# Expert results added into the residual in memory by indirect transfers, instead of stored, gathered back and combined

## The reference, cut to what matters

```
x = x + gnn(layernorm(x)) + attention(layernorm(x))
h = layernorm(x)                                 # 1250 x 1024
w, e = top2(router(h))                           # two experts of 8 for every token, with weights
x = x + sum over k of w[:, k] * expert[e[:, k]](h)
```

## Time and profile before

| | us |
|---|---|
| runs shown | 3441.88, 3448.74, 3455.16 (median 3448.74) |
| the profiled execution, its own time | 3453.75 |
| its span, first to last instruction | 3452.0 |
| PE busy, PE weight loads | 3101.3 (90%), 2834.2 (82%) |
| DVE, ACT, POOL busy | 2116.8, 1290.2, 401.6 |
| mean granted TensorE clock | 0.941 of full speed |

### The profile page before, as it was taken

The page is one execution under the profiler, slowest core; times in us unless marked ns, Lnnn a source line. Parts: engine busy times, 40 slices in busy tenths (PEclk is TensorE's granted clock), DMA queues, the critical chain, the costliest instruction groups (busy, mean ns, idle before and its releaser), DMA issues.

```text
span 3452.0 us, 52667 instructions
## 1 busy us (share of the span) xinstructions
PE 3101.3 (90%) x21876; PEld 2834.2 (82%) x21876; DVE 2116.8 (61%) x3710; ACT 1290.2 (37%) x2211; POOL 401.6 (12%) x302
## 2 busy tenths in 40 slices
PE   6999999989998799999489999989998999969992
PEld 6897797479987398888389997989998999968882
DVE  6985377977875744434556555776264734646664
ACT  4462055544421034333244334444044413325551
POOL 1044443442000100000300000000000000010002
PEclk9999999999998899999699999999999999969996
DMA  7322123122032156534641000452321432248777
GB/s 248 106 54 40 1 62 92 1 48 68 13 88 88 46 158 190 173 128 152 187 142 38 26 27 30 122 146 76 81 88 48 115 72 81 63 133 267 258 257 228
DMA packets 284267, 366.09 MB, mean 106 GB/s; under 512 B 52472, under 2 KB 234782, under 8 KB 282224
## 3 DMA queue, kind: packets, MB, share of 16 engines
q1 hardware_dynamic: 165035, 203.54, 20.0%
q0 software_dynamic: 51248, 68.03, 8.5%
q10 hardware_dynamic: 67717, 90.69, 8.1%
HBM read 285.75 MB, written 83.74 MB: 107 GB/s over the span
## 4 chain that ended last, share of the span: by engine, by line
PE 55%; DVE 4%; DMA 2%; ACT 2%; issue 1%; ACTq 1%; POOL 1%; POOLq 0%; DVEq 0%; SPq 0%
PE PV L459 12%; PE PV L460 12%; PE PV L461 12%; PE PV L563 6%; PE PS L459 3%; PE PS L461 3%; PE PS L460 3%; DMA b<-y_d,gidx 1%; PE PA L594 1%; PE PA L487 1%; DVE b L1848 1%; DVE b_split L1634 1%; ACTq L121 1%; ACT b L1248 1%; PE PA L878 1%
## 5 line engine op out<-in xcount | busy, mean ns | idle before, releaser
L459 PE MATMUL PV<-WH,b_split 128*125 128x256 f32 (+2 forms) x3708 | 1091.1, 294 | 124.6 <-DVE b_split L1634 107.7
L460 PE MATMUL PV<-WH,b_split 128*125 128x256 f32 (+2 forms) x3708 | 1077.4, 291 | 0.0
L461 PE MATMUL PV<-WH,b_split 128*125 128x256 f32 (+2 forms) x3708 | 1076.4, 290 | 0.0
L1634 DVE TENSOR_TENSOR b_split<-b,b_split 128x500 fp32r<-128x500 f32 x1040 | 687.4, 676 | 435.5 <-ACT b_split L1237 422.4
L1237 ACT CAST b_split<-b 128x500 fp32r<-128x500 f32 x1040 | 626.0, 612 | 808.8 <-PE PV L461 733.4
L459 PEld LDWEIGHTS PV<-WH,b_split 128*125 128x125 f32 (+2 forms) x3708 | 703.6, 190 | 149.7 <-issue 105.8
L460 PEld LDWEIGHTS PV<-WH,b_split 128*125 128x125 f32 (+2 forms) x3708 | 706.5, 191 | 9.9
L461 PEld LDWEIGHTS PV<-WH,b_split 128*125 128x125 f32 (+2 forms) x3708 | 703.0, 190 | 11.3
L1617 DVE TENSOR_TENSOR WH<-WS,WH 128x1024 fp32r<-128x1024 f32 x292 | 344.3, 1221 | 145.7 <-ACT WH L1222 144.4
L1222 ACT CAST WH<-WS 128x1024 fp32r<-128x1024 f32 x292 | 292.1, 1051 | 180.4 <-PE PV L563 143.4
L459 PE MATMUL PV<-b_split,WH 128*128 128x250 f32 (+3 forms) x1136 | 336.9, 297 | 9.2 <-DVE b_split L1634 6.4
(11 more groups left out here) (271 smaller groups left out, 3775.4 us busy)
## 6 DMA issues: line engine op xcount, KB each, us to landing
WS<-in_L_ffn_w SPq DMA_DIRECT2D x46, 1024.0 KB, 6.8
WH<-at_d SPq DMA_DIRECT2D x15, 1093.8 KB
WS<-in_L_ffn_gate_w SPq DMA_DIRECT2D x16, 1024.0 KB, 5.4
WS<-in_L_ffn_up_w SPq DMA_DIRECT2D x16, 1024.0 KB, 6.1
WS<-in_L_ffn_down_w SPq DMA_DIRECT2D x16, 1024.0 KB, 5.1
y_d<-b ACTq DMA_DIRECT2D x60, 256.0 KB
y_d<-b ACTq DMA_DIRECT2D x64, 196.0 KB
b<-key_d POOLq DMA_DIRECT2D x4, 2560.0 KB, 9.4
```

The source lines that it names most:

```text
L459: pe.matmul(o, a[0], b[0], start=start, stop=False, **kw)
L460: pe.matmul(o, a[0], b[1], start=False, stop=False, **kw)
L461: return pe.matmul(o, a[1], b[0], start=False, stop=stop, **kw)
L1634: ve.tensor_tensor(lo, src, hi.bitcast(F32), ALU.subtract).then_inc(xl_done, 1)
```

## The change

It does these things:

- `y_d`, the gathers L1202, `combine` and the result stores L1393 go. So do the four result buffers, the fill of `y_d` on SP's queue (L1020 to L1022), `store_x2` and the output stores at the end.
- The residual is first stored to memory: `store_normed` also stores each residual tile to `acc[layer]`, which is `x2_d` in layer 0 and the output itself in layer 1 (20 more issues on ACT's queue per layer).
- Results are weighted as they leave PSUM: DVE (`tensor_scalar`) and ACT (`activation` with a scale) multiply by `wslot`, the weight of each slot, into a ring of eight tiles of 4 KB a row, which takes the residual's place in SBUF.
- POOL adds each whole tile into `acc[layer]` by an indirect transfer with an add. It waits for both halves of the tile and for the landing of the previous transfer, since two slots may hold the same token. Empty slots go to 128 spare rows behind the tokens.
- The gather for block b + 2 now stands on POOL ahead of the adds of block b and behind those of block b - 1. In layer 1's conditional blocks POOL also waits for each block's last add and gather to land.
- `row_tokens` gets 20 more matmuls (plain float32) for `wslot`, and six more DVE instructions around them for that and for `sidx`, the target rows.
- In layer 0 ACT waits for all adds and loads the residual back into SBUF in ten transfers, and `ln_x2` waits for its group's load instead of combining.

The diff, cut to its core:

```diff
@@ -342,18 +344,14 @@
-        def y_slot(layer, n):
-            s = n % YRING[layer]
-            if layer == 1:
-                at = B3 + s * D
-            elif s >= 4:
-                return rbf[0:R, (s - 4) * D:(s - 3) * D]
-            elif n < 12:
-                at = B1 + (6 + s) * D
-            else:
-                at = (PTO, PTO + D, B1 + 8 * D, B1 + 9 * D)[s]
-            return F[0:R, at:at + D]
+        def y_number(layer, b, t):
+            return b * 4 + t if layer == 0 else E * 4 + b * 2 + t
+        def y_tile(layer, n):
+            at = (B3, B1)[layer] + n % YRING * D
+            return F[:, at:at + D]
@@ -576,7 +574,13 @@
                 mm.then_inc(v_full, 1)
-                mark["rows", layer] = v.n
+                bank = v.take(pe)
+                pe.wait_ge(weight_hot_ready, layer + 1)
+                for n in range(2 * NT):
+                    mm = pe.matmul(bank[0:r, 0:blocks * tiles], at_row[:, n, :].bitcast(F32),
+                                   at_weight[:, n, :], start=(n == 0), stop=(n == 2 * NT - 1))
+                mm.then_inc(v_full, 1)
+                mark["weights", layer] = v.n
@@ -1017,9 +1021,6 @@
-            for r0 in range(FIXED[1] * 256, BLK * 256, 1024):
-                r1 = min(r0 + 1024, BLK * 256)
-                sp.dma_start(y_d[1][r0:r1, :], A["x"][0:r1 - r0, :]).then_inc(y_filled, 16)
@@ -1097,10 +1098,6 @@
                     block(b)
-            for i in range(NT):
-                sp.wait_ge(yg_used, 2 * NT + 2 * (i + 1))
-                spread(sp, out[i * R:(i + 1) * R, :], rows(B1)[:, i, :], out_stored)
-            sp.wait_ge(out_stored, BOTH * NT)
@@ -1176,32 +1175,47 @@
+                npiece = tiles * D // HALF
+                def scatter(b):
+                    for t in range(tiles):
+                        n = y_number(layer, b, t)
+                        for half in range(2):
+                            j = (0 if layer == 0 else E * 8) + b * npiece
+                            j += half * tiles + t if layer == 0 else 2 * t + half
+                            pool.wait_ge((v_free, s_free)[j % 2], y_at[j])
+                        if n != y_number(layer, 0, 0):
+                            pool.wait_ge(y_st[(n - 1) % YRING], 16 * ((n - 1) // YRING + 1))
+                        c = b * tiles + t
+                        pool.indirect_dma_start(out=acc[layer],
+                                                out_offset=bass.IndirectOffsetOnAxis(ap=sidx[0:r, c:c + 1], axis=0),
+                                                in_=y_tile(layer, n)[0:r, :], in_offset=None, compute_op=ALU.add)\
+                            .then_inc(y_st[n % YRING], 16)
+                def added(b):
+                    n = y_number(layer, b, tiles - 1)
+                    pool.wait_ge(y_st[n % YRING], 16 * (n // YRING + 1))
                     used = pool.value_load(eblk[0:1, BLK:BLK + 1], min_val=0, max_val=BLK)
-                for b in range(min(FIXED[layer] + 1, blocks)):
-                    gather(b)
-                for b in range(FIXED[layer] + 1, blocks):
-                    with pool.If(used > b - 1):
-                        gather(b)
-                pool.wait_ge(route_ready, layer + 1)
-                if layer == 1:
-                    pool.wait_ge(y_filled, 16 * NFILL)
-                def results_stored(pieces):
-                    for q in range(4):
-                        pool.wait_ge(y_st[q], 16 * pieces // 4)
-                results_stored(E * 8 + layer * FIXED[1] * 4)
+                gather(0)
+                gather(1)
+                pool.wait_ge(acc_init[layer], BOTH * NT)
+                pool.wait_ge(v_free, mark["weights", layer] - 1)
+                for b in range(FIXED[layer]):
+                    if b + 2 < blocks:
+                        gather(b + 2)
+                    scatter(b)
+                added(FIXED[layer] - 1)
                     with pool.If(used > b):
-                        results_stored(E * 8 + (b + 1) * 4)
-                for n in range(2 * NT):
-                    i, k = divmod(n, 2)
-                    if n >= YRING[layer]:
-                        pool.wait_ge(yg_used, 2 * NT * layer + n - YRING[layer] + 1)
-                    pool.indirect_dma_start(out=y_slot(layer, n), out_offset=None, in_=y_d[layer],
-                                            in_offset=bass.IndirectOffsetOnAxis(ap=gidx[0:R, k, i:i + 1], axis=0))\
-                        .then_inc(yg_full[layer][n % YRING[layer]], 16)
+                        if b + 2 < blocks:
+                            gather(b + 2)
+                        scatter(b)
+                        added(b)
+                        if b + 2 < blocks:
+                            pool.wait_ge(xe_full[b % 2], 16 * (4 * 4 + tiles * ((b + 2) // 2 + 1)))
@@ -1325,6 +1339,7 @@
                     spread(act, xn_d[i * R:(i + 1) * R, :], xn_tile(layer, i), xn_rt[b])
+                    spread(act, acc[layer][i * R:(i + 1) * R, :], rows((B3, B1)[layer])[:, i, :], acc_init[layer])
@@ -1351,11 +1366,12 @@
                 if layer == 1:
-                    act.wait_ge(y_filled, 16 * NFILL)
                     turned_bank(0, k)
+                act.wait_ge(acc_init[layer], BOTH * NT)
+                act.wait_ge(v_free, mark["weights", layer])
@@ -1384,15 +1400,12 @@
                             continue
-                        if j >= 4:
-                            act.wait_ge(y_st[j % 4], 16 * (j // 4))
-                        act.copy(ffn_y(layer, j % 4)[0:r, :], s.read(act)[0:r, :]).then_inc(s_free, 1)
-                        for jj, pp, done in ((j - 1, p - 1, v_free), (j, p, s_free)):
-                            nd, t = divmod(pp, tiles) if layer == 0 else (pp % 2, pp // 2)
-                            act.wait_ge(done, y_at[jj])
-                            act.dma_start(y_d[layer][(b * tiles + t) * r:(b * tiles + t + 1) * r,
-                                                     nd * HALF:(nd + 1) * HALF],
-                                          ffn_y(layer, jj % 4)[0:r, :]).then_inc(y_st[jj % 4], 16)
+                        half, t = divmod(p, tiles) if layer == 0 else (p % 2, p // 2)
+                        n, c = y_number(layer, b, t), b * tiles + t
+                        if n >= YRING:
+                            act.wait_ge(y_st[n % YRING], 16 * (n // YRING))
+                        act.activation(y_tile(layer, n)[0:r, half * HALF:(half + 1) * HALF], s.read(act)[0:r, :],
+                                       ACT.Copy, scale=wslot[0:r, c:c + 1]).then_inc(s_free, 1)
@@ -1511,16 +1524,11 @@
             experts(0)
-            def store_x2(j):
-                g = j - NPIECE
-                if not 0 <= g < NB:
-                    return
-                act.wait_ge(yg_used, 4 * (g + 1))
-                spread(act, x2_d[2 * g * R:2 * (g + 1) * R, :].rearrange("(t p) d -> p t d", p=R),
-                       rows(B3)[:, 2 * g:2 * g + 2, :], x2_stored)
+            for q in range(YRING):
+                act.wait_ge(y_st[q], 16 * (E * 4 // YRING))
+            for g in range(NB):
+                spread(act, rows(B3)[:, 2 * g:2 * g + 2, :],
+                       x2_d[2 * g * R:2 * (g + 1) * R, :].rearrange("(t p) d -> p t d", p=R), x2_back[g])
@@ -1763,7 +1770,19 @@
                                      each(rowno[0:R, 0:r], HOTS), ALU.is_equal).then_inc(hot_ready, 1)
-                emptied(ve.tensor_copy(tidx[0:r, 0:w], v.read(ve)[0:r, 0:w]))
+                bank = v.read(ve)[0:r, 0:w]
+                vacant = rbf[0:r, 448:448 + w]
+                ve.tensor_scalar(tidx[0:r, 0:w], bank, -1.0, 0.0, ALU.add, ALU.max).then_inc(tidx_ready, 1)
+                d(ve.tensor_scalar(vacant, bank, 0.0, dumpt[0:r, 0:1], ALU.is_equal, ALU.mult))
+                d(ve.tensor_tensor(at_weight, past[:, :, 0:w], past[:, :, 1:], ALU.subtract))
+                d.sync()
+                ve.tensor_tensor(at_weight, at_weight,
+                                 wide(wk[0:R, :, :].rearrange("p k i -> p (k i)"), w), ALU.mult)\
+                    .then_inc(weight_hot_ready, 1)
+                d(ve.scalar_tensor_tensor(out=vacant, in0=vacant, scalar=-1.0, in1=bank, op0=ALU.add, op1=ALU.add))
+                d.sync()
+                emptied(ve.tensor_copy(sidx[0:r, 0:w], vacant))
+                ve.tensor_copy(wslot[0:r, 0:w], v.read(ve)[0:r, 0:w]).then_inc(v_free, 1)
@@ -1815,9 +1836,12 @@
                         if j % 2 == 0:
-                            if j >= 4:
-                                ve.wait_ge(y_st[j % 4], 16 * (j // 4))
-                            emptied(ve.tensor_copy(ffn_y(layer, j % 4)[0:r, :], v.read(ve)[0:r, :]))
+                            half, t = divmod(p, tiles) if layer == 0 else (p % 2, p // 2)
+                            n, c = y_number(layer, b, t), b * tiles + t
+                            if n >= YRING:
+                                ve.wait_ge(y_st[n % YRING], 16 * (n // YRING))
```

(62 more changed lines are left out.)

11 lines of the change are left out of this document (2 added, 9 removed).

## The result

The changed kernel takes **3429.19 us** in the median of 5 runs (3427.97 to 3433.35), beside 3448.74 before; the ratio is 0.9949, 95% interval 0.9932 to 0.9965. That is 19.5 us faster, inside the range of the forecast (3366 to 3432), and a third of the 60 that it promised. The profiled execution's span is 3426.6 us, against 3452.0.

The account below looks back on a forecast made before the run. PE was taken to bound the kernel nearly everywhere except the tails behind both layers' routed blocks. Layer 1's end -49.8, layer 0's end -15 and contention +5 sum to -60, giving 3389 us, range 3366 to 3432.

Parts of the forecast that it names:

- P: One add's cycle on POOL, issue, landing and wait together: 7 us in layer 0, 8 in layer 1.
- Layer 1's end: Behind layer 1's last result: two adds of 8 us end at 3402.2 and no output store is needed; -49.8 us.
- Layer 0's end: Behind layer 0's last result: four adds, ten loads on ACT, no combines or residual stores, steady pace at 1761; -15 us.
- Inside the blocks: Both layers' routed blocks: copies, adds and moved gathers are covered; only DMA contention costs, taken as +5 us.
- Layer 1's gathers: Layer 1's blocks: gathers behind adds arrive 15 or 21.5 us into a block, needed at 23; covered, little to spare.
- late gathers: Rival: POOL's order delays gathers in the five conditional blocks by some 2 us each; 3399, chance 0.1.
- Contention: Layer 1's blocks: DMA share rises from 0.81 towards 1.0, +5 us; as rival, late weight loads, +30, 3414, chance 0.16.
- Ahead of the blocks: Before each layer's blocks: 20 more matmuls cost nothing, 4 us per layer if float32 is slower; residual stores at worst 5.
- The sum: Whole kernel: -49.8 - 15 + 5 = -60 us, forecast 3389 for the median.

Follow-up runs that it names:

- e2_hoist_l0: Changed kernel with layer 0's gathers issued three blocks ahead, in front of the adds, in place of two; 3398.91 us, ratio to before 0.9850.
- e9_before_reordered: Kernel before, with layer 0's gathers for block b + 2 waiting until block b - 1's results are stored, without adds; 3453.12 us, ratio 1.0012.
- e4_plain_write: Changed kernel with every add replaced by a plain indirect write; layer 1 then routed other rows, 14 blocks in place of 15; 3363.55 us, ratio to before 0.9741.
- e3_hoist_l1: Changed kernel with layer 1's gathers issued three blocks ahead, in front of the adds, in place of two; 3420.37 us, ratio to before 0.9915.
- e6_plain_l1_only: As e1_hoist_both, with layer 1's adds replaced by plain indirect writes while layer 0 still adds; 3374.53 us, ratio to before 0.9798.
- e1_hoist_both: Changed kernel with both layers' gathers issued three blocks ahead, in front of the adds, in place of two; 3385.14 us, ratio to before 0.9820.

## Why the prediction was right or wrong

- **P, right.** I took 7 in layer 0 and 8 in layer 1. The last four adds of layer 0 are 6.4 to 6.7 apart (inside its blocks 6.6 to 9.4, median 7.55), and the 15 pairs in layer 1 have a median of 8.0 (7.1 to 12.2). The working fits too: of the 2.0 us between an add and a write 0.6 is issue, and 1.4 remain for the second pass of the data, for which I had 1.6 x 98/128 = 1.2.
- **Layer 1's end, right.** Forecast 13.7 us from the last result to the end (3402.2 - 3388.5), measured 15.9.
- **Layer 0's end, right in size.** Forecast -15, measured 100.0 in place of 119.7, -19.7. ACT's queue was over-priced. Its ten loads, in the timeline of ACT, took 4.7 us and not 12.7, so the root did not wait for them. From the last result to the first norm's end it was 33.4 us (forecast 39.2, before 26.5), and from there to the steady pace 26.5 less than before (forecast 28.5):

```profile
1699.70 0.33 ACTq L119 DMA_DIRECT2D b<-x_d  x1
...
1703.83 0.57 ACTq L120 DMA_DIRECT2D b<-x_d  x1
...
1709.27 0.20 ACT L1259 ACTIVATE b<-b 125x2 f32<-125x2 f32 x1 [3.55 <-DVE b L1674]
```

- **"Inside the blocks ... Layer 0 has 4 x 7 = 28 us of adds in blocks of some 57: covered": this is the step that failed.** I compared the adds' sum with the block's length, which only says that POOL's queue doesn't grow without bound. What counts is when the gather behind them is issued, against when PE wants its rows. In layer 0 PE starts to turn block b + 2 even ahead of block b's first result (block 5 at 1411.08 and block 3's result at 1420.47, before), earlier than I had placed it. That is 31.6 us behind block 2's last result (1379.50); with the adds in front, the rows of block 5 were there 35.1 us behind it (1425.96 - 1390.88). The price was +24.1 in the place of 0. e2_hoist_l0 takes it away, e9_before_reordered and e4_plain_write show that it takes the length of the adds and not the place alone.
- **Layer 1's gathers, same step, +17.3 in place of 0.** I had seen that the conditional blocks had "little to spare" (21.5 of 23) and priced it as the rival *late gathers* at +10, chance 0.1. At an add's cycle of 10 to 12, as in four of the 15 pairs, the reserve is gone; PE waited for gathered rows until 3139, 3345 and 3390, in all 12.1 us, the first time in a block that is always done. e3_hoist_l1 gives the block back its 283.6.
- **Contention, +5 forecast, none found.** The share rose towards 1.0 as forecast, to 0.92, and the blocks of layer 1 with adds and the gathers in order keep the old pace, 282.5 to 285.6 in seven profiles against 283.2. e6_plain_l1_only has a share of 0.81 and gains some 1 us inside the block (282.7).
- **Ahead of the blocks.** Layer 0's first result came at 1255.8, 1.1 earlier. In layer 1 the plain float32 matmuls cost 2 of the up to 4 us that I had bounded.
- **The sum.** In the profiles -1.1 + 24.1 - 19.7 + 1.5 + 17.3 - 47.7 = -25.6 against the spans' -25.4. With the order put right (e1_hoist_both) the kernel runs at 3385 to 3389 in two series; the forecast was 3389. That match is in part luck: its profile has 7.2 us less in layer 0's block than before, which I had not forecast and cannot explain, and its layer-1 tail gives 42.5 and not 49.8.

## What to carry to other kernels

When a chain of waiting transfers is put into a queue, don't compare its sum with the period: write down for the transfer behind it when it is issued now, when it will be, and when its reader wants it. Issue what feeds the bound engine ahead of what merely drains results, and deepen the prefetch by one stage if the buffer allows it. Where a queue is going to wait for a landing anyway, short issues belong inside that wait.

## What the runs showed of the hardware

- At the end of layer 0 an indirect add of 98 rows of 4 KB into HBM has a cycle of 6.7 us with a wait for each landing, a plain indirect write 4.7. POOL's issue is 1.53 us for the one and 0.94 for the other, at the same number of rows; 1.55 was the issue with 4-byte rows too, so the longer issue goes with the add and not with the row's length.
- The DMA bytes in the profile are the same for adds and for plain writes (21.1 MB, gathers included), while the queue's busy share is 45.5% against 29.3%.
- With the hoist, layer 0's block became shorter than before the change: 389.8 to 393.9 us in eight profiles, where the kernel before and e9_before_reordered have 397.9 and 397.3. Both of those have a PE wait of 3.8 and 4.1 us for a weight cast, and the kernel before shows a granted clock of 0.83 around it (1400 to 1420) where e1_hoist_both has 1.00. The change took the result stores away from ACT and the DMA queues, but this alone does not give the 7 us: e4_plain_write has no such stores either and took 399.9, only 1.4 of it a wait for gathered rows. The cause stays open.
